# A state-space scan with a mixture of experts on one core: the copy that keeps scan states moves from GpSimd to VectorE

## The reference

```
dA = jnp.exp(delta[..., None] * A)
dBu = delta[..., None] * Bm[:, :, None, :] * u[..., None]
def step(h, inp):
    dA_t, dBu_t, C_t = inp
    h = dA_t * h + dBu_t
    y = jnp.einsum('bdn,bn->bd', h, C_t)
    return (h, y)
```

## Time and profile before

| what | us |
|---|---|
| median of 3 runs | 754.57 (752.45 to 755.8) |
| the profiled execution | 750.72 |
| its span, first to last instruction | 748.4 |
| scan, first to last (58.3 to 530.4) | 472.2 |
| segment 4, from its first scan to that of segment 5 | 62.4 |
| segment 5, the same | 60.5 |

### The profile page before, as it was taken

One profiled execution on the slowest core, in us unless ns is written; L12 is line 12 of the kernel. 1 busy time (PEld: TensorE's weight loads), 2 busy tenths in 40 slices (PEclk: granted clock), 3 DMA queues, 4 the chain that ended last, 5 costly groups with the idle time before them and its releaser, 6 DMA issues.

```text
span 748.4 us, 14748 instructions
## 1 busy us (share of the span) xinstructions
PE 641.6 (86%) x4563; PEld 536.3 (72%) x4563; DVE 550.4 (74%) x1170; ACT 539.0 (72%) x1024; POOL 542.4 (72%) x519
## 2 busy tenths in 40 slices
PE   4878889989888989979988976999687998899995
PEld 3434766867657757757766766889577888799984
DVE  4257598899888898987989987999534574355553
ACT  3269989979969997996997997868226644366540
POOL 3148989988999899999999999978615455444432
PEclk9999999999999999999999997999889999999997
DMA  7030534638445334533454333686011222122544
GB/s 221 7 108 4 164 94 109 165 88 255 122 113 143 108 102 135 155 98 98 106 139 130 96 95 106 165 204 162 20 35 56 59 60 64 56 68 63 150 154 155
DMA packets 65196, 82.93 MB, mean 111 GB/s; under 512 B 6960, under 2 KB 55152, under 8 KB 61024
## 3 DMA queue, kind: packets, MB, share of 16 engines
q1 hardware_dynamic: 59648, 70.78, 34.8%
q0 software_dynamic: 4320, 9.12, 3.6%
q10 hardware_dynamic: 1152, 2.10, 0.7%
HBM read 52.19 MB, written 29.78 MB: 110 GB/s over the span
## 4 chain that ended last, share of the span: by engine, by line
PE 44%; ACT 28%; issue 10%; DVE 9%; POOL 5%; another core or an unknown queue 2%; DMA 2%; SPq 0%; ACTq 0%; DVEq 0%; POOLq 0%
PE psum L575 26%; PE psum L579 17%; ACT S L999 9%; ACT dA L1010 8%; DVE ring L1363 3%; POOL ring L550 3%; POOL S L530 1%; ACT xn L902 1%; ACT L937 1%; ACT soft L930 1%; ACT soft L929 1%; ACT soft L937 1%; ACT L1010 1%; ACT hT L884 1%
## 5 line engine op out<-in xcount | busy, mean ns | idle before, releaser
L550 POOL TENSOR_TENSOR ring<-ring,Cb 128x1024 f32<-128x1024 f32 x128 | 303.0, 2369 | 16.6 <-DVE ring L1363 11.3
L1010 ACT ACTIVATE dA<-delta,A 128x512 f32<-128x512 f32 x256 | 178.4, 715 | 12.5 <-DVE ring L1363 10.4
L579 PEld LDWEIGHTS psum<-ident,S 128*128 128x128 f32 x896 | 105.4, 143 | 113.6 <-issue 78.1
L579 PE MATMUL psum<-ident,S 128*128 128x128 f32 x896 | 139.8, 280 | 45.1 <-issue 24.1
L579 PE MATMUL psum<-ident,ring 128*128 128x128 f32 x1088 | 162.5, 281 | 11.1 <-DMA ring<-results 5.4
L1363 DVE TENSOR_TENSOR_SCAN ring<-dA,psum 128x512 f32<-128x512 f32 x128 | 150.5, 1206 | 11.7 <-PE psum L579 7.8
L1363 DVE TENSOR_TENSOR_SCAN ring<-dA,state,psum 128x512 f32<-128x512 f32 x128 | 158.0, 1266 | 1.4 <-PE psum L579 1.0
L999 ACT ACTIVATE S<-duT,BT 128x256 f32<-128x256 f32 x320 | 139.3, 501 | 27.2 <-DVE duT L1106 22.4
L567 POOL DMA_INDIRECT results<-xn,result_at x71 | 68.7, 967 | 107.7 <-DVE xn L1495 61.7
L579 PEld LDWEIGHTS psum<-ident,ring 128*128 128x128 f32 x1088 | 130.9, 145 | 12.5 <-DMA ring<-results 5.7
L575 PE MATMUL psum<-uT,S 128*128 128x128 f32 x852 | 110.6, 281 | 0.6 <-issue 0.5
(11 more groups left out here) (229 smaller groups left out, 814.0 us busy)
## 6 DMA issues: line engine op xcount, KB each, us to landing
Cb<-c_rows SPq DMA_DIRECT2D x32, 1024.0 KB, 6.1
token_rows<-zeros SPq DMA_DIRECT2D x64, 272.0 KB, 7.0
uT<-token_rows SPq DMA_DIRECT2D x71, 68.0 KB
ring<-results SPq DMA_DIRECT2D x8, 512.0 KB, 3.5
xT<-in_xT SPq DMA_DIRECT2D x4, 512.0 KB, 5.0
out_T<-xT ACTq DMA_DIRECT2D x8, 256.0 KB
stage<-in_xT SPq DMA_DIRECT2D x6, 256.0 KB, 8.5
gateup_w<-in_gate SPq DMA_DIRECT2D x1, 1408.0 KB, 9.9
```

Source lines behind the costliest of these rows:

```text
L550: nc.gpsimd.tensor_tensor(ring[:, k % RING], ring[:, k % RING], Cb[:, group_ % 2, own, :].unsqueeze(1).to_broadcast([P, HALVES, BANK]), AL ...
L579: return nc.tensor.matmul(out, block_in, ident[at, at], is_transpose=True, start=start, stop=True, skip_group_check=True)
L1010: nc.scalar.activation(dA[:, (k * HALVES + a) % DA_SLOTS, :], delta[:, s % 2, a, :], ACT.Exp, scale=A[:, a, n:n + 1]).then_inc(da_ready, 1)
```

## The change

The copy of L546 leaves GpSimd. A function `keep(k)` does it on VectorE, called for k - 1 right behind scan(k, 0). GpSimd's wait on the semaphore `kept` stays in front of the product. There are 64 copies, as before.

```
@@ gpsimd
                 pool.wait_ge(scanned, (k + 1) * HALVES)
                 if s % SEG == 0:
-                    nc.gpsimd.tensor_copy(state[:, n, :], ring[:, k % RING, :, BANK - 1]).then_inc(kept, 1)
                     pool.wait_ge(kept, s // SEG * NSTATE + n + 1)
@@ vector
+            def keep(k):
+
+                s, n = divmod(k, NSTATE)
+                if s % SEG == 0:
+                    dve.wait_ge(scanned, (k + 1) * HALVES)
+                    V.tensor_copy(state[:, n, :], ring[:, k % RING, :, BANK - 1]).then_inc(kept, 1)
...
                 scan(k, 0)
+                if k > 0:
+                    keep(k - 1)
                 gap_work(2 * n, s)
                 scan(k, 1)
```

## The result

The changed kernel takes 767.8 us (median of 6 runs, 764.46 to 768.83) where the kernel before took 755.12 in the same session (6 runs, 752.45 to 756.65): ratio 1.0164, 95% interval 1.0137 to 1.019, so 1.6% slower. The forecast was 766.2. The profiled execution took 767.72, its span 765.1. Of the 16.7 us between the two spans 13.8 lie in the scan, which now lasts from 57.5 to 543.5 us. The other 2.9 lie outside of it: the expert stage behind the scan, which no part of the change touches, took 3.6 us more, what stands ahead of the scan 0.7 less. The expert stage took 218.0 to 223.9 us in the thirteen profiled executions of this study, and why is open. The medians differ by 12.7 us; the profiled execution of the kernel before was a short one, 750.72.

The account below looks back on a forecast made before the run. GpSimd was taken to set the pace in segments 2 to 6 from state 5 on, VectorE at segment starts. Three segments at 3.3 us plus 1.7 for segment 0 gave 11.6 on 754.57: 766.2 us, range 757.0 to 772.0.

Parts of the forecast that it names:

- Rival 3: Even segments: GpSimd's pace decides everywhere, early steps have slack, freed time comes back; 7.2 us less, 747.4; chance 0.07.
- The new wait at step 68: Segment 4: product 68 must wait for scan (69,0) and the copy behind it, starting 1.85 us later.
- Step 76: Segment 4: product 76 waits for scan (77,0), which sits behind duT; 0.8 us more.
- Segment 0: Scan (10,0) comes late, so product 9 comes 3.5 us later; 1.7 us taken as reaching segment 1.
- The block of 0.7 us at step 64: Segment 4's start: the copy is held through GpSimd's scatter and S, so VectorE stands 0.7 us.
- So the gain of 0.26 us a step is gone: Steps 69 to 75: held copy delays the product some 0.25 us behind S, what GpSimd's own copy cost; no gain.
- rival 1: VectorE's copy is not held at all: 0.7 us a segment, 3.3 us in all, 757.9; chance 0.18.
- rival 2: Copy is held but gets its turn between product k-1 and S: 1.3 us a segment, 760.2; chance 0.13.
- Copies of "0.1 to over 2 us": Sign of being right: VectorE's copies last this long and end 0.04 us behind a GpSimd instruction's end.
- rival 4: Held copies also delay VectorE's work for others, 3 us more in three segments; TensorE's clock could drop; 775; chance 0.07.
- Step 79: End of segment 4: loses 0.3 us to a late scan behind uT; left out of the sum.
- The sign of being wrong as a whole: Time outside of the scan, 58 to 530 us, moves by more than 2 us.

Follow-up runs that it names:

- experiment 8: Kernel before without GpSimd's copy and both waits on it, states filled with zeros once: 747.4 us, ratio 0.9909.
- experiment 1: Kernel before, its copy still on GpSimd, which also waits for the next scan (k+1,0) in front of it: 769.69 us, ratio 1.0224.
- experiment 5: Changed kernel with extra transposes of the identity filling TensorE's idles before it waits for S, at five steps: 760.58 us, ratio 1.0094.
- experiment 11: Changed kernel with both a maximum in place of VectorE's copy and TensorE's idles filled: 760.18 us, ratio 1.0071.
- experiment 2: Kernel before plus 64 VectorE copies from another tile into a spare one, behind the next scan, for which nobody waits: 789.22 us, ratio 1.0468.
- experiment 4: Changed kernel with VectorE's copy moved to the end of step k, ahead of scan (k+1,0): 757.82 us, ratio 1.0068.
- experiment 7: Changed kernel with a maximum over one column in place of the copy, at the end of the step ahead of the next scan: 752.53 us, ratio 0.9988.
- experiment 3: Changed kernel with a maximum over one column (same values) in place of VectorE's copy: 764.51 us, ratio 1.0149.
- experiment 9: Experiment 7 with TensorE's longer idles filled by 10 to 14 extra transposes at each of ten steps: 751.04 us, ratio 0.9948 to the kernel before.
- experiment 10: Experiment 2 with a maximum over one column in place of each extra copy: 754.92 us, ratio 1.0004 to the kernel before.

## Why the prediction was right, and where it was not

The forecast of 766.2 and the measured 767.8 agree, and so does the sign. The terms agree only in part, and it is luck that two errors cancelled: a loss that was missing (the clock) against a block that didn't come and a gain that did.

- **What bounds the kernel.** Right. Taking GpSimd's copy away brings segment 4 from 62.4 to 60.2 us (experiment 8), which only an engine on the path can do. Rival 3's 747.4 is also experiment 8's time, which is chance: that kernel has no copy at all.
- **The new wait at step 68**: 1.85 forecast, 1.84 measured, and 1.81 with the wait alone (experiment 1). **Step 76**: 0.8 forecast, 0.74 measured, and 0.95 with the wait alone. These two could be worked out to a tenth because every piece stood in the trace: the end of scan (k + 1, 0), and what the product had followed.
- **Segment 0**: 1.7 forecast, 2.4 measured, 2.0 with the wait alone. Product 9 came 4.0 us later (forecast 3.5). The mechanism held, the share that reaches segment 1 was too small.
- **The odd segments stay as they were**: right, within 0.1 us.
- **The block of 0.7 us at step 64**: wrong. Copy 64 took 0.14 us at the end of a scatter, ahead of S, and product 64 came 0.27 us sooner than before. I had treated scatter and S as one stretch that holds VectorE until its end; the copy had its turn between the two.
- **"So the gain of 0.26 us a step is gone"**: this step failed. The copy is of a form that GpSimd holds, as the earlier trace rows had it, but at a small price: 0.2 to 0.4 us on 19 copies, 0.4 us in segment 4 (experiments 5 and 11). The gains of steps 69 to 78 did come back, 1.3 us in segment 4 by product starts. Without the clock's part the change would have cost segment 4 1.6 us (experiment 5), which is neither the forecast's 3.3 nor rival 1's 0.7, but close to rival 2's 1.3; in all, experiment 5's 760.6 stands beside rival 2's 760.2. Rival 2's mechanism was at work as well: the copies got their turn between product and S, and products 69, 70, 72 and 74 of the changed kernel started as their S ended. The forecast had set S first.
- **Copies of "0.1 to over 2 us"**: the longest was 0.58. Over 2 us they are only in experiments 2 and 4, in which the next product doesn't wait for them.
- **The term that was missing**: TensorE's clock. The forecast said that S of step 71 would be 1.85 us later and that TensorE waits for it, and mentioned a lower clock in rival 4 in passing, without a price. It should have gone on: the idle of 1.29 us becomes 2.35, and behind idles of 2.1 to 3.6 us the kernel before already had stretches at the lower level, one in each of segments 2 to 5 and more in segment 6. It could have been priced as a risk, not as a certainty: idles of 2.11 us in segments 3 and 5 of the changed kernel and of 2.19 us in experiment 7 were not followed by one. The clock's part in segment 4 is 2.6 us, nearly as much as the whole forecast for it. Experiment 5 takes 7.2 us off by it alone (5.3 by the two ratios, as the kernel before ran 1.2 us faster in that session).
- **Step 79**: 0.3 us, worked out and then left out of the sum; it is 0.6, and it does reach segment 5.
- **The sign of being wrong as a whole**, over 2 us outside of the scan, did come: 2.9 us. The expert stage alone differs by up to 5.9 us between profiled executions whose code for it is the same, so a limit of 2 us says nothing here; the segments put the loss of the scan into the even ones.

So the forecast's 3.3 us a segment were 2.65 of waits that came as foreseen, and 0.7 of a block that didn't occur, with no gain. In segment 4 there came 3.2 of waits and 2.6 of clock, less 1.3 of gain and less the 0.3 by which the first scan of segment 5 is ahead of the products. What stays open: whether the hold has a part in where the clock falls (experiments 3 and 11 differ in segment 4 by 1.5 us, both with maxima, the filling being the one difference; the changed kernel and experiment 3 differ by 1.5 at step 79, the hold being the one difference), and what makes the expert stage differ from one execution to the next.

## What to carry to other kernels

When work moves to another engine, ask behind which instruction it stands there: here a place behind the next scan cost 12 us more than one ahead of it (experiments 3 and 7), and the move to VectorE by itself, with the maximum, nothing (experiment 7). A small copy within the state memory on VectorE beside a busy GpSimd is better written as a reduce over one element. And when a delay makes TensorE idle longer, price the matmuls behind the idle at the lower clock too, if the trace shows such stretches behind idles of that length.

## What the chip showed that I had not expected

- A copy of 128x2 values on VectorE lasted up to 2.26 us beside GpSimd's product (experiment 2), and through an S and the product behind it up to 2.74 us (experiment 4). Where nothing holds it, it takes 0.14. It got its turn between a product and an S that was ready in 40 of 40 cases (34 in experiment 2, 6 in the changed kernel), and between an S and a product that was ready in none of three (experiment 4). A reduce of the same values took 0.12 to 0.16 us in all of its 320 instances (experiments 3, 7, 9, 10 and 11).
- A scatter of GpSimd (1.0 us) holds such a copy only in a part of it: those that came up 0.08 to 0.30 us after its start took 0.14 to 0.16 us, those that came up 0.35 to 0.66 us after it lasted until its end, 0.33 to 0.64 us, and those that came up at 0.80 us or later took 0.13 to 0.22 us (the changed kernel, experiments 2, 4 and 5).
- A granted clock of 0.50 followed idles of TensorE of 2.35 and 1.60 us, and cost 1.4 and 1.2 us on the path, while it stayed at 1.00 behind an idle of 2.19 us in experiment 7. In the kernel before, the same level in segments 2 to 5 cost nothing that filling the idles could win back (753.3 against 753.9 us, the segments within 0.1).
- 58 useless transposes at five steps win more (5 to 7 us) than removing the hold does (3.3 us, or 1.1 by the ratios).
